# Head products of two steps issued together in the state-space stage of a two-layer kernel

## The reference

```python
proj = input_states @ in_proj_w.T                 # gate, x/B/C, dt
xBC  = silu(conv4(xBC) + conv_b)                  # causal convolution over 4 tokens, per channel
scores  = einsum(C, B) * Ldec * dt                # 8 groups of 16 heads of 64 channels, state of 128
y_intra = einsum(scores, x)
states  = einsum(dt * dlast, B, x)                # carried from chunk to chunk
y_inter = einsum(C * exp(cum), prev)
y = y_intra + y_inter + D * x
g = y * silu(gate); g = g * rsqrt(mean(g*g over a group) + eps) * norm_w
return g @ out_w.T
```

## Time and profile before

| | |
|---|---|
| median of 3 runs | 2087.34 us (2086.0 to 2087.62) |
| the profiled execution | 2088.12 us, its span 2086.4 us |
| mean granted TensorE clock | 0.998 |
| state-space stage, first to last head product | 557.3 to 1725.1 us of the span |
| busy: TensorE, VectorE, ScalarE, GpSimd | 2057.9, 1466.8, 1335.4, 868.3 us |
| start of one group's first entry, and of the next one's | 1001.26 us, 1151.74 us |

### The profile page before, as it was taken

The page is one execution under the profiler, slowest core; times in us unless marked ns, Lnnn a source line. Parts: engine busy times, 40 slices in busy tenths (PEclk is TensorE's granted clock), DMA queues, the critical chain, the costliest instruction groups (busy, mean ns, idle before and its releaser), DMA issues.

```text
span 2086.4 us, 33789 instructions
## 1 busy us (share of the span) xinstructions
PE 2057.9 (99%) x12040; PEld 1550.7 (74%) x12040; DVE 1466.8 (70%) x1815; ACT 1335.4 (64%) x2376; POOL 868.3 (42%) x758
## 2 busy tenths in 40 slices
PE   7999999999999999999999999999999999999999
PEld 6655554688877777877777777777777777888887
DVE  4566666486678878778688787787787786555556
ACT  4255555536678788787887887878778783232332
POOL 1011111130357657667566675666666672000000
PEclk9999999999999999999999999999999999999999
DMA  5523222243545454544545555455455467554452
GB/s 185 169 59 86 76 74 56 86 136 95 158 147 179 146 166 158 168 147 164 169 151 159 162 162 158 153 158 172 145 173 163 149 209 256 149 151 142 145 187 86
DMA packets 182782, 305.35 MB, mean 146 GB/s; under 512 B 20416, under 2 KB 96704, under 8 KB 182496
## 3 DMA queue, kind: packets, MB, share of 16 engines
q1 hardware_dynamic: 182624, 303.29, 46.5%
HBM read 249.90 MB, written 53.06 MB: 145 GB/s over the span
## 4 chain that ended last, share of the span: by engine, by line
PE 90%; DVE 5%; ACT 2%; POOL 1%; issue 1%; DMA 1%; SPq 0%; DVEq 0%; POOLq 0%; ACTq 0%
PE ssm_pp L156 16%; PE ssm_pp L158 15%; PE ssm_pp L157 15%; PE att_gu L686 6%; PE ssm_py L1478 5%; PE ssm_py L1473 4%; PE ssm_pstate L1457 4%; DVE stk_mx L351 3%; PE ssm_turn L1434 2%; PE att_rows L341 2%; PE ssm_py L156 1%; PE ssm_py L158 1%; PE ssm_py L157 1%; PE down_ps L156 1%; PE down_ps L158 1%; PE down_ps L157 1%
## 5 line engine op out<-in xcount | busy, mean ns | idle before, releaser
L156 PE MATMUL ssm_pp<-xhi,ssm_lo 128*128 128x512 f32 x1192 | 478.8, 402 | 0.9 <-DVE ssm_bc L1720 0.4
L158 PE MATMUL ssm_pp<-xhi,ssm_hi 128*128 128x512 f32 x1192 | 465.5, 391 | 0.0
L157 PE MATMUL ssm_pp<-xlo,ssm_hi 128*128 128x512 f32 x1192 | 464.9, 390 | 0.0
L1605 ACT ACTIVATE ssm_sct<-ssm_cumb,ssm_gpar 128x128 f32<-128x128 f32 x1024 | 313.0, 390 | 55.5 <-PE ssm_py L1478 49.4
L148 POOL TENSOR_TENSOR ssm_lo<-ssm_raw,ssm_hi 128x512 fp32r<-128x512 f32 x146 | 238.8, 1641 | 77.8 <-ACT ssm_hi L137 77.8
L156 PEld LDWEIGHTS ssm_pp<-xhi,ssm_lo 128*128 128x128 f32 x1192 | 223.6, 188 | 63.6 <-issue 19.0
L1720 DVE SCALAR_TENSOR_TENSOR ssm_xc<-ssm_pp,vectors,ssm_xc 128x1022 f32<-128x1022 f32 (+2 forms) x192 | 245.2, 1277 | 23.6 <-ACT ssm_xc L1559 18.9
L158 PEld LDWEIGHTS ssm_pp<-xhi,ssm_hi 128*128 128x128 f32 x1192 | 223.8, 188 | 48.1
L157 PEld LDWEIGHTS ssm_pp<-xlo,ssm_hi 128*128 128x128 f32 x1192 | 224.0, 188 | 42.6
L1755 DVE TENSOR_TENSOR ssm_sct<-ssm_sct,ssm_cbm 128x1024 f32<-128x1024 f32 x128 | 229.3, 1792 | 26.5 <-ACT ssm_sct L1612 26.5
L1908 POOL TENSOR_TENSOR ssm_go<-ssm_t,ssm_gt 128x512 f32<-128x512 f32 x128 | 167.3, 1307 | 169.2 <-DVE ssm_t L1791 169.2
(11 more groups left out here) (288 smaller groups left out, 4135.1 us busy)
## 6 DMA issues: line engine op xcount, KB each, us to landing
ssm_cumb<-dt_sums SPq DMA_DIRECT2D x96, 1024.0 KB, 5.7
ssm_raw<-w SPq DMA_DIRECT2D x150, 256.0 KB, 3.7
gated<-ssm_go SPq DMA_DIRECT2D x128, 256.0 KB, 2.6
ssm_cumb<-dt_sums SPq DMA_DIRECT2D x32, 512.0 KB, 4.0
ssm_gt<-w SPq DMA_DIRECT2D x64, 256.0 KB, 2.7
ssm_xc<-gated SPq DMA_DIRECT2D x32, 512.0 KB, 4.2
ssm_sct<-gated SPq DMA_DIRECT2D x32, 512.0 KB, 4.3
ffn_raw<-w SPq DMA_DIRECT2D x37, 256.0 KB, 2.8
```

Of the source, the lines that this page charges most:

```text
L156: pe.matmul(out, wlo, xhi, start=start, stop=False)
L157: pe.matmul(out, whi, xlo, start=False, stop=False)
L158: return pe.matmul(out, whi, xhi, start=False, stop=stop)
L1605: i = act.activation(sct[:, s % 2, h, :], cumb[:, s % 2, 0, h, :], ACT.Relu, scale=-1.0, bias=gpar[:, unit, 0, s % NTOK, h:h + 1])
```

## The change

TensorE: `scan` ends after the state's product; its head products become `outputs(g, s)`, and odd steps issue `outputs(g, s - 1)` and `outputs(g, s)` one after the other, even steps none. VectorE: `finish` of steps s - 2 and s - 1 both in even steps, ahead of `grown` and `scores`. ScalarE: in odd steps `lags(s + 1)` come behind `square(s - 2)` and a silu that stood behind it, in even steps the order stays. GpSimd: `output` of s - 2 instead of s - 1, `add_squares` of s - 3 instead of s - 2, `decay` behind `output` in odd steps, `weigh` always last. SyncE: `write` of s - 2. The ends of the stage get the calls left over.

```diff
@@ sync
-                    if before(g, s, 1):
-                        write(*before(g, s, 1))
+                    if before(g, s, 2):
+                        write(*before(g, s, 2))
...
+            write(G - 1, NS - 2)
             write(G - 1, NS - 1)
@@ tensor, scan
                     squares(unit)
+
+            def outputs(g, s):
+                ch = s % NC
                 pe.wait_ge(xp_done, g * NS + (s + 1))
@@ tensor, body
                     scan(g, s)
+                    if s % 2 == 1:
+                        outputs(g, s - 1)
+                        outputs(g, s)
                     for e in at(s, last)[1:]:
@@ scalar, body
-                    if behind(g, s, 1, last):
+                    if s % 2 == 0:
                         lags(*behind(g, s, 1, last))
                     if before(g, s, 2):
                         square(*before(g, s, 2))
...
+                    if s % 2 == 1 and behind(g, s, 1, last):
+                        lags(*behind(g, s, 1, last))
                     if behind(g, s, 1, last):
                         decays(*behind(g, s, 1, last))
@@ vector, body
                     if before(g, s, 1):
                         advance(*before(g, s, 1))
+                    if s % 2 == 0 and before(g, s, 2):
+                        finish(*before(g, s, 2))
+                        finish(*before(g, s, 1))
                     grown(g, s)
                     scores(g, s)
-                    if before(g, s, 1):
-                        finish(*before(g, s, 1))
...
+            finish(G - 1, NS - 2)
             finish(G - 1, NS - 1)
@@ gpsimd, body
-                    decay(g, s)
-                    if before(g, s, 1):
-                        output(*before(g, s, 1))
-                    ahead = last and s >= HALF_AT
-                    if ahead and behind(g, s, 1, last):
-                        weigh(*behind(g, s, 1, last))
+                    if before(g, s, 3):
+                        add_squares(*before(g, s, 3))
+                    if s % 2 == 0:
+                        decay(g, s)
                     if before(g, s, 2):
-                        add_squares(*before(g, s, 2))
-                    if not ahead and behind(g, s, 1, last):
+                        output(*before(g, s, 2))
+                    if s % 2 == 1:
+                        decay(g, s)
+                    if behind(g, s, 1, last):
                         weigh(*behind(g, s, 1, last))
             passes(pool, body)
+            add_squares(G - 1, NS - 3)
+            output(G - 1, NS - 2)
             output(G - 1, NS - 1)
```

## The result

The changed kernel takes 2269.34 us (2263.43 to 2270.06, 4 runs), the kernel before 2086.67 beside it: ratio 1.0872, 95% interval 1.0857 to 1.0886. That is 183 us more. The forecast was 2186, 99 more, and its range ended at 2226. The sign, the kind of wait and most places were right. The size was not.

What follows compares the result with a forecast made beforehand. TensorE bounds the kernel. Waits of 15.3 less 2.6 gained give +12.7 a group, 89 for seven groups; the last group adds 8.6 and the end 1: +99, 2186 us, range 2143 to 2226.

Steps and rivals of the forecast that it cites:

- What bounds the kernel: TensorE, busy 99% of the span: time comes only from shortening its stream and is lost where it must wait.
- The joined run gains 0.32: On TensorE, joining two head-product runs saves 0.32 us a pair (0.24 to 0.35), 20 us for 64 pairs.
- Convolutions come too late for their slots: TensorE's entries wait for late last readers of `ssm_pp` slots: seven waits, 15.3 us a group (11.5 to 19.8).
- x5, x6, x7, C, x2 and x3: Waits ahead of entries 16, 18, 20, 23, 28 and 29: 2.7, 2.0, 2.5, 0.7, 1.5 and 3.3 us a group.
- The step that failed first: Claim that the other engines finish earlier work before T, so a group's waits simply add to 15.3 us.
- T: Moment when the first head products of a joined pair are done, with some 7 us of work newly ahead.
- a piece that costs nothing: GpSimd's `output` and ScalarE's `square` one step later: no cost, at most 1 us in x5's and x2's chains.
- the range's 139: Upper end of the forecast loss over the whole kernel: +99, from 65 to 139 us.
- The last group and what follows: Last group +8.6 us (3.5 to 16), and 1 (0 to 3) behind the stage.
- only the drains count: Rival: slots' readers are on time and 64 x 0.32 = 20 us are gained, 2067. Chance 0.06.
- The contention case: Rival: all VectorE two-input operations take their long durations beside GpSimd's round, +139, 2226. Chance 0.12.
- entry 25: In step 9, entry 25 waits 2.6 us (1.2 to 3.9) for x0's convolution, set by VectorE's queue.

Runs made afterwards that it cites:

- l0_before_light: Kernel before with two of VectorE's three convolution taps left out: 2083.9 us, ratio 0.9989.
- w3: Kernel before with the head products of steps 6 and 7 alone joined, in groups 0 to 6: 2083.91 us, ratio 0.9988.
- e1: Changed kernel with x7's first_tap moved ahead of the late lags in odd steps: 2265.52 us, ratio 1.0859.
- v1: Changed kernel with taps ahead of lags and lone entries of odd steps tapped and convolved in their own step: 2206.57 us, ratio 1.058.
- e2: Changed kernel with GpSimd's output of step 7 made in step 8 instead of step 9: 2242.26 us, ratio 1.0754.
- v2: Changed kernel with v1's early taps and own-step convolutions plus e2's early output of step 7: 2173.66 us, ratio 1.0416.
- p10_pad: Kernel before with 10 small VectorE memsets ahead of x0's convolution in step 10 of groups 0 to 6: 2108.76 us, ratio 1.0107.
- p24_pad: Kernel before with 24 small VectorE memsets ahead of x0's convolution in step 10 of groups 0 to 6: 2156.47 us, ratio 1.0334.
- w4: Kernel before with the four pairs of steps 0 to 7 joined in groups 0 to 6, with v1's early taps and convolutions there: 2078.23 us, ratio 0.9968.
- v3: v2 plus own-step convolutions for even steps' lone entries, decays ahead of squares in even steps, output ahead of decay: 2166.32 us, ratio 1.0385.
- w1_last_pair: Kernel before with only the head products of steps 14 and 15 joined, in groups 0 to 6: 2101.22 us, ratio 1.0069.

## Why the prediction was half right

- **What bounds the kernel**: right. TensorE's stream alone counts. l0_before_light took 2.6 us off every convolution and gained 0.1%.
- **The joined run gains 0.32**: right, 0.33 in steps 0 and 1, and 0.32 in w3's group (150.49 to 150.17). The drain at the change of tiling that the Trainium skill names ("TensorEngine Tiling (Array Packing)", Key Properties) would be a part of these 0.32; no run tells it from the rest of a run's start and end.
- **Convolutions come too late for their slots**: right in place and in price for x5, x6, x7, C, x2 and x3, by the table. The way, through late lags and taps, is shown by e1 for x7, and for x5, x6 and C by v1, where earlier taps and convolutions took away the waits ahead of entries 16, 18 and 23.
- **The step that failed first** was the sentence "The helpers are through with what precedes T before T comes, so the waits don't feed each other, and they add." In step 9 ScalarE wasn't through, because of output(7), which I had put down as a piece that costs nothing. I followed `output` to its own buffer and to the square, not to the `ssm_gt` that the next group's gate overwrites. 3.5 us in each of 7 groups: 25 of the 82 missing between the profiled executions (spans of 2267.6 and 2086.4, 181 more, against 99). e2 shows it. The same sort of queue made entry 30 wait 0.8, 6 in all; that one is read from the traces of the changed kernel and v2, not tried alone.
- **The term that was missing** is TensorE's clock. The words "they add" also took a wait as its own length. Per group 6.2 us more were lost at the lower level, 43 in 7 groups, the larger part of the miss, and 1.3 beyond the waits' printed length, 9 in all. Without these 52 the 181 would be 129, inside the range's 139; without the 31 of the step above they would be 150 and still outside. p10_pad and p24_pad show the clock's part without any joined product.
- **The last group and what follows** took 14.3 more, against 10 forecast. Of these 3.6 are one wait of a state's product for ScalarE's copy of the sums, 4.23 where the kernel before has 0.59. From the last group's first entry to the end, before and changed:

```profile
1603.20:2086.40 483.20, 476.12 (x2419) 385.13 (x2417) 306.71 (x350) 208.51 (x329) 97.15 (x82) 1.00 0.53 164
1770.12:2267.64 497.52, 477.85 (x2419) 387.43 (x2417) 307.58 (x354) 210.31 (x329) 96.61 (x85) 0.99 0.50 160
```

- **The rivals**: that only the drains count was wrong for the changed kernel and is right for w4. The contention case had the bound nearest to the result by accident: VectorE's waits were not longer than forecast.

Together, in the profiled executions: 99 + 25 (entry 25) + 6 (entry 30) + 43 (clock) + 9 (beyond the printed waits) - 6 (the six other waits came to 0.9 a group less) + 4 (last group and behind) + 2 (the seven groups before it took 166.9 more, not 7 x 23.6) = 182, against 181 measured.

What stays open: when the lower clock follows a wait. The same wait in the same kernel is followed by it in some groups and not in others. And why e1's group, and the changed kernel's, take 174.1 both: that the lower clock ate just what the wait gave back is measured; why so exactly isn't settled. I also didn't separate in v1 to v3 what each move does.

## What to carry to other kernels

If a stream bound by one engine is rearranged, list for each instruction that comes later everything that it releases, write-after-read of the next round's buffers included, and for each that comes earlier or falls away what it stood in front of. A gain of 0.3 us a pair is worth having only where both neighbours have slack; join those alone, as w4 does. And price a wait of TensorE at more than its length: at 1.3 to 1.5 times in p24_pad and p10_pad (71 for 54, 23 for 15).

## What the hardware did unexpectedly

- A single wait of 2.1 us brought TensorE to 1.2 GHz behind it in four of six groups of p10_pad, 0.43 for 512 columns instead of 0.23, at a price of 1.7 us on top (a group of 154.3 is 3.8 over 150.5). In the two others the same wait cost its length and 0.1.
- A wait of 1.9 did so in two of six groups of w1_last_pair, and ahead of entry 18 in every group of e1_tap_first but only in the first of the changed kernel.
- Taking one wait out of eight (2.5 us a group) changed the group's time by 0.03 us, the mean granted clock going from 0.95 to 0.94.
